# The first two layers of a four-layer network reordered: two tiles turned by TensorE instead of DMA, and a first weight chunk that is scaled and split ahead of the others

## The reference

```python
x = x + attn0(layernorm(x))      # for each of 512 positions, 4x4 scores between the batch entries
x = x + ffn0(layernorm(x))       # x W' + b, top-2 gate over 8 experts, rank-16 adapters
x = x + attn1(layernorm(x))      # 32-head causal attention with low-rank queries and keys
x = x + ffn1(layernorm(x))       # x W' + b and rank-16 adapters weighted by a softmax router
```

```python
q = transpose(x, (2, 0, 1))                       # l, n, c
scores = einsum('lnc,lmc->lnm', q, q) / sqrt(512)
msg = einsum('lnm,lmc->lnc', softmax(scores), q)
return x + transpose(msg, (1, 2, 0))              # x is the normalized input here
```

```python
result = x @ W_base.T + b_base
probs = softmax(x @ W_gate.T); the two largest, divided by their sum, are the route weights of 8 experts
h = einsum('bnd,erd->bner', x, A) * route_w
return result + einsum('bner,eor->bno', h, B)     # SCALING is 1
```

## Time and profile before

| | |
|---|---|
| runs | 1632.85, 1630.63, 1631.84 us, median 1631.84 |
| profiled execution | 1631.13 us, span 1629.3 us, mean granted clock of TensorE 0.992 |
| TensorE busy | 1547.9 us, 95% of the span |
| VectorE, ScalarE, POOL busy | 1018.8, 868.9, 811.3 us |
| block `first` | 0 to 171.3 us |
| block `lora_layer0` | 171.3 to about 404 us |

### The profile page before, as it was taken

The page is one execution under the profiler, slowest core; times in us unless marked ns, Lnnn a source line. Parts: engine busy times, 40 slices in busy tenths (PEclk is TensorE's granted clock), DMA queues, the critical chain, the costliest instruction groups (busy, mean ns, idle before and its releaser), DMA issues. The chain is left out here.

```text
span 1629.3 us, 31927 instructions
## 1 busy us (share of the span) xinstructions
PE 1547.9 (95%) x12366; PEld 950.2 (58%) x12366; DVE 1018.8 (63%) x2747; ACT 868.9 (53%) x1654; POOL 811.3 (50%) x699
## 2 busy tenths in 40 slices
PE   5898899999989999999999999889999999999998
PEld 4655455555556776777777777644444444465554
DVE  7898857776778888888888888832110010344433
ACT  6886222221759999999999999931210000211110
POOL 4223244444957888888888888830010000244440
PEclk9999899999999999999999999999999999999999
DMA  9894334444756999999998999997763331233331
GB/s 359 297 330 149 91 88 107 143 142 128 154 120 112 187 173 189 179 184 187 195 190 174 184 185 173 178 208 226 176 167 80 101 91 26 75 66 84 83 86 65
DMA packets 560263, 249.82 MB, mean 153 GB/s; under 512 B 502256, under 2 KB 535152, under 8 KB 559984
## 3 DMA queue, kind: packets, MB, share of 16 engines
q1 hardware_dynamic: 560112, 247.78, 66.1%
HBM read 73.68 MB, written 48.23 MB: 75 GB/s over the span
## 5 line engine op out<-in xcount | busy, mean ns | idle before, releaser
L1967 POOL TENSOR_TENSOR xb<-xb 128x1280 f16<-128x1280 f32 x128 | 335.6, 2622 | 7.8 <-ACT xb L1870 7.8
L1862 ACT ACTIVATE xb<-bk,D_sv,qw_c 128x512 f32<-128x512 f32 (+3 forms) x512 | 289.3, 623 | 4.4 <-DVE D_sv L1925 4.2
L1916 DVE TENSOR_REDUCE bk<-bk 128x1 f32<-128x512 f32 (+3 forms) x512 | 228.3, 492 | 20.5 <-PE bk L1812 19.9
L92 POOL TENSOR_SCALAR mv<-mv 128x1 f32<-128x1 f32 x64 | 31.2, 488 | 279.1 <-DVE mv L87 278.1
L1870 ACT ACTIVATE xb<-xb 128x1280 f16<-128x1280 f32 x128 | 162.7, 1271 | 13.1 <-DMA xb<-xb 9.3
L1803 PE MATMUL bk<-kTh,D_QTh 128*128 128x512 f16 (+3 forms) x512 | 153.4, 300 | 6.3 <-ACT xb L1862 6.2
L1804 PE MATMUL bk<-kTl,D_QTh 128*128 128x512 f16 (+3 forms) x512 | 153.2, 299 | 0.0
L1805 PE MATMUL bk<-kTh,D_QTl 128*128 128x512 f16 (+3 forms) x512 | 146.5, 299 | 0.0
L1827 PE MATMUL D_t<-vh,xb 128*128 128x65 f16 x1280 | 131.5, 194 | 4.7 <-DMA xb<-xb 3.0
L1828 PE MATMUL D_t<-vl,xb 128*128 128x65 f16 x1280 | 131.6, 193 | 0.0
L1829 PE MATMUL D_t<-vh,xb 128*128 128x65 f16 x1280 | 131.0, 193 | 0.0
(11 more groups left out here) (331 smaller groups left out, 4383.9 us busy)
## 6 DMA issues: line engine op xcount, KB each, us to landing
od<-D_os SPq DMA_DIRECT2D x32, 512.0 KB, 4.5
xd<-xb SPq DMA_DIRECT2D x16, 512.0 KB, 4.2
ow_raw<-mwd SPq DMA_DIRECT2D x16, 512.0 KB, 4.7
xb<-xd SPq DMA_DIRECT2D x16, 512.0 KB, 5.9
out_x<-xb SPq DMA_DIRECT2D x16, 512.0 KB, 3.0
xb<-in_x SPq DMA_DIRECT2D x6, 1024.0 KB, 13.6
A_wo<-in_wo SPq DMA_DIRECT2D x6, 1024.0 KB, 7.5
ow_raw<-in_w SPq DMA_DIRECT2D x16, 384.0 KB, 4.3
```

The lines of the kernel that those rows point to most:

```text
L1862: m = e.activation(p[:, AT[i]:AT[i] + N], Sb[n % 4][:, c:c + N], ACT.Exp, scale=qw.col(qw.NEG, g), bias=s[:, 7 - i:8 - i])
L1916: m = e.tensor_reduce(minima(u, i), Sb[n % 4][:, c:c + N], AX.X, ALU.min)
L1967: e.tensor_tensor(P2[u % 3][:, 1280:2560], P[u % 3][:, :], P2[u % 3][:, 0:1280], ALU.subtract).then_inc(s_pl, 1)
```

## The change

It changes the first two blocks and nothing behind them.

1. Tile 15 of the first layer is normalized by VectorE, no longer by ScalarE; tile 1 of the second by ScalarE (`Norm.ON`).
2. The first three unlike pairs of j = 0 and of j = 1 are multiplied before the last four tiles are there; the order of `pairs` is by the second index.
3. The totals are taken in two matmuls: the first four parts after message (5, 0), and their scale early, the other ten after message (7, 2). ScalarE squares the last four parts behind the loop; chunk 0 is split before the other totals are there.
4. Tiles 0 and 1 of the second layer are turned by TensorE in float32 (eight transposes into two banks); ScalarE evicts the high half and VectorE subtracts for the low half. Their `act_high`, `pool_low` and `sp_turn` go.
5. The bias is loaded in the first block (into the memory of a normalized tile); POOL adds it to tile 0 there, and VectorE to tile 1 in the next block.
6. Second layer: gate(0) is VectorE's first work, `finish(0)` moves ahead of the statistics of tile 3, gate(2) ahead of those of tiles 4 and 5, and TensorE's order of the first three tiles is new. ScalarE's `qw.act_high` moves to the head of an iteration.

```diff
-    ON = "da" * 8 + "d" * 19 + "a" * 13 + "d" * 16
+    ON = "da" * 7 + "ddda" + "d" * 17 + "a" * 13 + "d" * 16
...
+    HAND = 2
...
     def pe_turned(self, w, n):
-        w.wait_ge(self.s_ft[n % 4], 16 * (n // 4 + 1))
+        if n < self.HAND:
+            w.wait_ge(self.s_lo, n + 1)
+        else:
+            w.wait_ge(self.s_ft[n % 4], 16 * (n // 4 + (n % 4 >= self.HAND)))
+
+    def pe_turn(self, e, w, n, banks, s_tr):
+
+        h = self.at(self.hb, n)
+        self.norm.applied(w, N_F0 + n)
+        w.wait_ge(self.s_lo, n)
+        for q in range(2):
+            for k in range(4 * q, 4 * q + 4):
+                i = e.matmul(banks[q][:, 128 * (k - 4 * q):128 * (k - 4 * q) + 128], h[:, 128 * k:128 * k + 128], self.ident,
+                             start=True, stop=True, is_transpose=True)
+            i.then_inc(s_tr, 1)
+
+    def act_turned_high(self, e, w, n, banks, s_tr, before, s_q):
+        for q in range(2):
+            w.wait_ge(s_tr, before + 2 * n + q + 1)
+            e.activation(self.at(self.hT, n)[:, 4 * q:4 * q + 4, :], banks[q][:, :].rearrange("p (k c) -> p k c", k=4),
+                         ACT.Copy).then_inc(self.s_hi if q else s_q, 1)
+
+    def dve_turned_low(self, e, w, n, banks, before, s_q):
+        t = self.at(self.hT, n)
+        w.wait_ge(s_q, before + n + 1)
+        for q in range(2):
+            if q:
+                w.wait_ge(self.s_hi, n + 1)
+            i = e.tensor_tensor(t[:, KD + 4 * q:KD + 4 * q + 4, :], banks[q][:, :].rearrange("p (k c) -> p k c", k=4),
+                                t[:, 4 * q:4 * q + 4, :], ALU.subtract)
+        i.then_inc(self.s_lo, 1)
...
-                if (j, c) == (7, 0):
+                if (j, c) == (5, 0):
                     w.wait_ge(s_we, 8)
                     w.wait_ge(norm.s_half, 2)
-                    lw.pe_totals(e, w, ones, wb[0])
-
-        for t in range(2):
-            feed.pe_turned(w, t)
-            w.wait_ge(s_tot, 2)
-            lw.pe_columns(e, w, feed.halves(t), wb[t], 0).then_inc(s_c, 1)
+                    lw.pe_totals(e, w, ones, wb[0], 0, 4)
+                if (j, c) == (7, 2):
+                    w.wait_ge(s_tot, 2)
+                    lw.pe_totals(e, w, ones, wb[0], 4)
+                    w.wait_ge(s_me, 2 * NT)
+                    feed.pe_turn(e, w, 0, mb, s_tr)
+
+        feed.pe_turned(w, 0)
+        w.wait_ge(s_tot, 4)
+        lw.pe_columns(e, w, feed.halves(0), wb[0], 0, range(0, 4))
+        feed.pe_turn(e, w, 1, mb, s_tr)
+        lw.pe_columns(e, w, feed.halves(0), wb[0], 0, range(4, KD)).then_inc(s_c, 1)
+        feed.pe_turned(w, 1)
+        lw.pe_columns(e, w, feed.halves(1), wb[1], 0).then_inc(s_c, 1)
...
-        feed.act_high(e, w, 0)
-        for n in range(2):
-            w.wait_ge(s_msg, 28)
+        for n in (10, 11):
+            lw.act_square(e, w, n)
+        w.wait_ge(s_msg, 28)
+        for n in range(4):
             lw.act_split(e, w, n)
-        for n in range(2, 4):
-            lw.act_split(e, w, n)
-        feed.act_high(e, w, 1)
+        for n in (12, 13):
+            lw.act_square(e, w, n)
+        feed.act_turned_high(e, w, 0, mb, s_tr, 2 * NT, s_hT)
+        w.wait_ge(lw.s_sq, lw.N)
+        feed.act_apply(e, w, 1, xb[:, row(1), :])
+        feed.act_turned_high(e, w, 1, mb, s_tr, 2 * NT, s_hT)
         for n in range(4, 8):
             lw.act_split(e, w, n)
...
-        for n, m in apart:
+        for j in range(2):
+            for n, m in apart[:3]:
+                product(j, n, m)
+        for n, m in apart[3:]:
             product(0, n, m)
...
+                if (j, c) == (6, 2):
+                    lw.dve_first_total(e, w, wb[0], s_tot)
+                if (j, c) == (7, 0):
+                    lw.dve_split(e, w, 0)
                 add(j, c)
                 if (j, c) == (7, 0):
                     w.wait_ge(s_add, 29)
                     norm.dve_stats(e, w, N_F0, xb[:, row(0), :])
-                    lw.dve_totals(e, w, wb[0], s_tot)
+                    lw.dve_split(e, w, 1)
+                    feed.dve_apply(e, w, 0, xb[:, row(0), :])
                 elif (j, c) == (7, 1):
-                    feed.dve_apply(e, w, 0, xb[:, row(0), :])
                     norm.dve_stats(e, w, N_F0 + 1, xb[:, row(1), :])
+                elif (j, c) == (7, 2):
+                    lw.dve_other_totals(e, w, wb[0], s_tot)
+                    feed.dve_turned_low(e, w, 0, mb, 2 * NT, s_hT)
+                    lw.dve_split(e, w, 2)
...
-        lw.dve_split(e, w, 0)
-        feed.dve_apply(e, w, 1, xb[:, row(1), :])
-        for n in range(1, 4):
-            lw.dve_split(e, w, n)
+        lw.dve_split(e, w, 3)
+        feed.dve_turned_low(e, w, 1, mb, 2 * NT, s_hT)
         lw.dve_all_inverses(e, w, 1.0)
...
-    ORDER = [("c", 0, 1), ("c", 1, 1), ("w", 0), ("c", 0, 2), ("w", 1), ("a", 0), ("c", 1, 2), ("a", 1)]
-    for t in range(2, NT):
+    ORDER = [("c", 0, 1), ("c", 1, 1), ("w", 0), ("c", 0, 2), ("w", 1), ("c", 1, 2), ("a", 0), ("c", 2, 0), ("a", 1), ("c", 2, 1),
+             ("w", 2), ("c", 2, 2), ("a", 2)]
+    for t in range(3, NT):
...
-        for n in range(8, 10):
+        lw.act_split(e, w, 8)
+        gate_exp(0)
+        for n in range(9, 12):
             lw.act_split(e, w, n)
         feed.act_high(e, w, 2)
-        gate_exp(0)
-        for n in range(10, 12):
-            lw.act_split(e, w, n)
+        high_w(0)
         gate_exp(1)
-        high_w(0)
...
         for t in range(2, NT):
+            if QW < t <= QW + 8:
+                qw.act_high(e, w, t - QW - 1)
             gate_exp(t)
...
-            if QW < t <= QW + 8:
-                qw.act_high(e, w, t - QW - 1)
...
+        gate(0)
+        w.wait_ge(s_xb, 1)
+        e.tensor_tensor(xb[:, row(1), :], xb[:, row(1), :], bias[:, :], ALU.add).then_inc(s_xb, 1)
+        lw.dve_split(e, w, 8)
         stats(2)
-        lw.dve_split(e, w, 8)
+        lw.dve_split(e, w, 9)
         apply(2)
-        lw.dve_split(e, w, 9)
-        gate(0)
...
         low_w(1)
+        finish(0)
         stats(3)
         apply(3)
-        stats(4)
-        finish(0)
         adapter(0)
         finish(1)
         adapter(1)
         for t in range(2, NT):
+            if t == 2:
+                gate(t)
+                stats(t + 2)
             stats(t + 3)
             apply(t + 2)
...
-            gate(t)
+            if t > 2:
+                gate(t)
```

102 lines of the change are left out of this document (62 added, 40 removed).

## The result

The changed kernel takes 1619.65 us (median of 6 runs, 1618.6 to 1623.11) against 1631.78 for the kernel before in the same session: a ratio of 0.9929, 95% interval 0.9919 to 0.9939. On another chip, beside the experiments, it took 1621.23 against 1630.84, ratio 0.9948 (0.9935 to 0.9962). I had forecast about 1621 (1621.2 in the sum), faster, in a range of 1613 to 1627. The profiled execution is the slowest of the first six: 1623.11 us, span 1621.3, which is 8.0 less than the span before; 12.1 is the difference of the medians.

The account below looks back on a forecast made before the run. TensorE, working in 95% of the span, was taken as the bound, with only idle time or a slow clock to win. 9.4 + 1.0 = 10.4 us took 1631.1 to 1620.7 profiled, 1621.2 as a median; range 1613 to 1627.

Parts of the forecast that it names:

- part 3: Seam to the second layer: TensorE idle 1.7 us instead of 5.86 before the first columns; 5.9 won, shift included.
- part 4: First tiles of the second layer: totals after tile 3 at 218.8 us instead of 228.25, 9.4 won of 14.
- Part 1: First layer's last tile normalized by VectorE: last eviction ends at 37.9 us, 1.6 earlier; bounds 0 and 1.8.
- Part 2: Six products before the last tiles are there: worth 0 by themselves, at most 0.7 us.
- ScalarE's hold of 1.36 us: At 140.58 us, end of the stretch to the last j: ScalarE holds TensorE for 1.36 us in both orders.
- rival B: TensorE's clock falls more often, around 154 and 177 us: two more falls and no 1.6 won early; 1626 us; chance 0.20.
- The chain: Second layer, from apply(4) through POOL's bias add and finish(2) to gate(3) at 211.5 us; TensorE waits 3.0 for it.
- Part 5: ScalarE's high half of the query weights moved to the head of an iteration: 1.0 us won, bounds 0 and 4.
- A: VectorE isn't behind at tile 3, gate(3) waited for by less than 1 us: 14 to 16 won, 1616; chance 0.17.
- C: The gain is given back by a growing wait in the steady loop or the projections: 1631 us; chance 0.05.
- D: Slower: the lower clock, once fallen at 154 us, stays through many short idle times; up to 1647.5 us; chance 0.03.

Follow-up runs that it names:

- e1: Changed kernel with tile 15 of the first layer normalized by ScalarE again; 1622.59 us, ratio to the kernel before 0.9939-0.9964.
- e2: Changed kernel with the six early products undone, products of j = 0 and then j = 1 in one go each; 1622.74 us, ratio to before 0.9933-0.9957.
- e8: Changed kernel with ScalarE evicting the fused weights ahead of its weighted sum in j = 6; 1619.11 us, ratio to before 0.9920-0.9948.
- e3: Changed kernel with ScalarE's high half of the query weights back at the end of an iteration; 1621.81 us, ratio to before 0.9927-0.9952.
- e7: Changed kernel with tiles 0 and 1 of the second layer turned by DMA again, POOL's work reordered; 1628.2 us, ratio to before 0.9976-0.9995.
- e4: Changed kernel with POOL adding the bias one tile ahead; 1619.14 us, ratio to before 0.9912-0.9937.
- e5: Changed kernel with bias adds one tile ahead, tile 2's placed earlier, and POOL waiting for VectorE's low half of the query weights; 1612.56 us, ratio to before 0.9884-0.9915.
- e6: Changed kernel with the second layer's first-tile orders as before on TensorE, ScalarE and VectorE, bias adds staying; 1621.28 us, ratio to before 0.9926-0.9954.

## Why the prediction was right

The number was right in part by luck: of the terms of its sum, part 3 gave 1.1 us less than forecast and part 4 gave 2.1 more, and the profiled execution then lost 3.1 us in the projections, for which the sum had no term. (In the sum itself 1620.7 + 0.7 makes 1621.4 as a median, not 1621.2.) Point by point:

- Part 1: -1.6 forecast, the last eviction ends at 38.01, -1.5; the part undone costs 1.7 up to 138 us (e1).
- Part 2: 0 forecast, 0 measured (e2). But "TensorE comes to the last j 1.7 us earlier" failed: the messages of j = 6 were to end at 145.2, and message (7, 0) starts at 146.15 (146.74 before). I had kept ScalarE's hold of 1.36 us as it was, with no loss behind it. TensorE came to it 2.5 us earlier (136.69 instead of 139.22) and waited 1.95; the group still started 1.9 earlier, no less than the 1.7 that I had asked for. What failed is the clock: it then fell in seven of nine executions (3.25 instead of 2.23 for the group, 2.33 instead of 1.99 for the next). That is the mechanism of rival B, 1.3 to 1.6 us, in a place that I hadn't named. It is curable (e8).
- Part 3: idle time of 1.7 forecast, 0.94 + 1.02 measured. The block's first columns come 4.76 earlier and not 5.9; the 1.1 missing is the fall of the clock just named (without it, as in e1 and e3, they would come 1.3 earlier). With the turns back on DMA the gain is gone (e7, with its own order of POOL's work).
- Part 4: of the 9.4 at the totals 3.5 were to come from the second layer's tiles themselves. It was 5.6. The chain was right in its links: the wait before its turn was 2.21 (forecast 3.0; TensorE came 0.8 later, for the reason above), and undoing one link, the bias add before finish(2), takes it away (e4, e5). That gate(3) ended within 0.05 us of the forecast is luck: the chain started 1.1 later than I had it (166.66, not 165.6) and was 1.1 shorter. That is one half of the 2.1 that I was off. The other is the lower clock behind the wait, 1.7 forecast, 0 measured: the columns behind it ran at 2.4 GHz in all seven executions that had it; about 0.7 of that went into a longer way from the turn to the totals (6.33 us instead of the 5.6 that I had without the clock), 0.5 of it a wait of 0.80 before the totals that was 0.27. And I had counted the new orders as part of the gain: e6 shows that they are worth 0.1. Of the 5.6, 3.7 are TensorE's busy time (49.31 to 45.56), the clock that no longer falls, and 1.9 idle time.
- Part 5: 1.0 forecast, 0.8 to 1.1 measured (e3), of which the table shows 0.5 because the idle time at the start of the projections was 1.65 instead of 1.06. VectorE's low half beside POOL is held nearly in full: 3.42 us for the one at 255.72, beside a bias add that starts at 255.71 and takes 2.35, 2.77 at the median, 1.28 alone. The Trainium skill, "SBUF — State Buffer", on the shared port pair, says that the loser blocks for the whole instruction; the trace is near to that (1.75 of 1.97 us in e4).
- Rivals: A did not come: gate(3) was waited for by 2.2 us, not by under 1. B's sign, two more stretches at 1.2 GHz between 150 and 200 us, did not come either; its mechanism came twice outside them, near 138 us and in the projections. C came in the profiled execution with 3.1 of 10.9 us, in the projections, where I had seen no slack but "DMA turns", and half of it was the clock. D had nothing for it: with sixteen transposes of tiles 0 and 1 between messages and columns the clock was 1.00 from 150 to 160 us, and from 166 to 200. The Trainium skill, "TensorE: Matmul & The Clock Gate", Part 4, says that transposes don't count as busy in the way that matmuls do; this trace shows no fall of the clock behind these. The trace of the kernel before differs from it: with nothing but transposes ahead, eight of them took 1.91 us at 15.49, and from 18.50 on 1.04 to 1.06, so the clock rose on transposes alone.

Sum of the terms: 1.6 + 4.3 + 3.5 + 1.0 = 10.4 forecast; 1.5 + 3.2 + 5.6 + 0.5 measured, 10.9 without rounding, at the start of the projections.

## What to carry to other kernels

When a long elementwise operation on POOL lies beside a chain of short ones on VectorE, count each of its microseconds as lost to the chain, whichever of the two is the one that matters; then look for the place where VectorE works from PSUM or waits anyway, and make POOL wait for that place (e5: one wait, and the bias adds one tile ahead, 8.7 us). An idle time of the bound engine that another engine's chain ends does not stay as it is when the bound engine comes earlier: here it grew by 0.6 of the 2.5 us won, and the clock behind it took 1.3 more. Before a gain is put down to a reordering, undo the reordering alone: here it was worth 0.1, with all the rest in place. And where idle time goes, compare the engine's busy time for the same work too: two thirds of that gain were the clock.

## What the runs showed of the hardware that I had not expected

- The same idle time of TensorE has different consequences. After 1.95 to 1.97 us near 138 us, ahead of fp32 matmuls, the clock fell in seven of nine executions. In streams of fp16 columns: after 2.2 us at gate(3) in none of seven (changed twice, e1, e2, e3, e7, e8: 6.33 or 6.34 us from the turn to the totals in each); after 2.07 us at the first turn in two of ten (e3, e7): e3 needs 52.79 for the stretch in which the like kernels need 51.16; after 2.3 to 2.6 us in the projections in five of seven. Such falls cost 1.2 to 1.8 us each. They would fit the spread of some 4 us between runs of one kernel; that they are its cause was not measured, since only one execution of each has a trace, and the mean granted clock of a run follows its time only in part (0.994 at 1623.11 us, 0.995 at 1618.6).
- POOL's long operation holds some of VectorE's instructions with SBUF sources whatever their size: a CAST of two elements took 2.31 us, a 128x1 subtraction 1.47, a normalization with one tensor source 2.52. Those with one source in PSUM (finish, adapter) weren't held. Nor was every one that reads only SBUF: the statistics beside POOL's bias add of 153.15 (2.36 us), and before, a reciprocal beside POOL's low half of 179.15 (2.12 us):

```profile
153.59 0.68 DVE L83 BATCH_NORM_STATS2 st<-xb 128x6 f32<-128x512 f32 x1
```

```profile
179.31 0.16 DVE L1369 RECIPROCAL F_sm<-F_sm 128x1 f32<-128x1 f32 x1
```
